# Causal mask of the exponentiated scores: sixteen extra contraction rows and a GpSimd select, replaced by one mask matmul for each diagonal block

## The reference, cut to what matters

```python
H, hd = 16, 16                        # B, T, D = 8, 1024, 256
q, k, v = split(h @ W_qkv)            # h: layer norm of x, scaled and shifted
attn = einsum('bhqd,bhkd->bhqk', q, k) / sqrt(hd)
attn = attn + where(key > query, -inf, -slope[h] * |key - query|)   # causal ALiBi
attn = softmax(attn, axis=-1)
x = x + ga * (einsum('bhqk,bhkd->bhqd', attn, v) @ W_out)
```

## Time and profile before

| | |
|---|---|
| median of 3 runs | 4325.94 us (4319.2 to 4332.71) |
| the profiled execution | 4325.94 us, its span 4324.2 us |
| busy in the span | PE 3432.9 us (79%), DVE 3542.9 (82%), ACT 2259.0 (52%), POOL 2620.2 (61%) |
| first and last `b_pT` score matmul | 306.0 and 1315.5 us |
| POOL selects L636 | 704 in number, 192.0 + 46.6 us busy |
| PE mask matmuls L676 | 1024, 218.3 us busy |

### The profile page before, as it was taken

How to read it: one execution, slowest core, us unless ns; L and a number is a source line. 1 busy time by engine, 2 the same in 40 slices (tenths; PEclk the granted TensorE clock), 3 DMA queues, 4 the chain that set the end, 5 groups by cost and what they waited for, 6 DMA issues and landing times. The chain is left out here.

```text
span 4324.2 us, 73212 instructions
## 1 busy us (share of the span) xinstructions
PE 3432.9 (79%) x22476; PEld 1607.5 (37%) x22476; DVE 3542.9 (82%) x5196; ACT 2259.0 (52%) x3974; POOL 2620.2 (61%) x2515
## 2 busy tenths in 40 slices
PE   5979999999994999999567777777777777777567
PEld 3634333344332555555222322222222222222156
DVE  5767777777754999999279999989999899998957
ACT  5626666666673333333355565656565555565422
POOL 1102222222221888887178888888898888888823
PEclk8979999999997999999778888778888888888589
DMA  4884554554522111110112222221222222212222
GB/s 146 285 153 67 82 78 66 79 81 66 82 38 80 35 47 42 46 45 25 47 43 53 67 52 66 63 49 47 66 67 56 66 53 67 56 50 46 53 86 86
DMA packets 274023, 300.44 MB, mean 69 GB/s; under 512 B 34560, under 2 KB 204663, under 8 KB 273623
## 3 DMA queue, kind: packets, MB, share of 16 engines
q1 hardware_dynamic: 273630, 295.68, 31.0%
HBM read 210.22 MB, written 84.51 MB: 68 GB/s over the span
## 5 line engine op out<-in xcount | busy, mean ns | idle before, releaser
L1684 POOL TENSOR_TENSOR d_dBu<-d_dtu,d_Bn 128x1024 f32<-128x1024 f32 x512 | 1202.9, 2375 | 184.9 <-DVE d_h L1751 184.8
L785 DVE TENSOR_REDUCE b_Gc<-b_pS 128x1 f32<-128x512 f32 (+4 forms) x1248 | 742.8, 644 | 228.7 <-PE b_pS L676 147.5
L1532 ACT ACTIVATE d_dA<-d_dt,d_decay 128x512 f32<-128x512 f32 x1024 | 690.2, 687 | 446.4 <-DVE d_h L1751 429.0
L758 ACT ACTIVATE b_P<-b_pT 128x512 f32<-128x512 f32 (+1 forms) x1120 | 572.3, 575 | 373.9 <-PE b_pT L664 371.7
L1751 DVE TENSOR_TENSOR_SCAN d_h<-d_dA,d_dBu 128x512 f32<-128x512 f32 x512 | 586.1, 1203 | 99.4 <-ACT d_dA L1532 92.2
L1751 DVE TENSOR_TENSOR_SCAN d_h<-d_dA,d_last_h,d_dBu 128x512 f32<-128x512 f32 x512 | 616.1, 1262 | 54.3 <-ACT d_dA L1532 51.4
L674 PE MATMUL b_pS<-KS,QS 99*128 99x512 bf16 (+3 forms) x1536 | 475.7, 339 | 47.6 <-DVE b_Gc L785 25.5
L636 POOL TENSOR_SCALAR_AFFINE_SELECT b_P<-b_P 128x128 f32<-128x128 f32 (+2 forms) x608 | 192.0, 323 | 527.5 <-ACT b_P L758 515.7
L664 PE MATMUL b_pT<-QS,KS 118*128 118x512 bf16 (+3 forms) x1536 | 450.8, 330 | 40.7 <-issue 21.3
L1758 DVE TENSOR_TENSOR d_h<-d_h,d_C 128x2048 f32<-128x2048 f32 x192 | 433.8, 2259 | 0.7 <-PE d_C L1415 0.7
L1487 PE MATMUL d_f<-d_xnT,w_inT 128*128 128x512 f32 x512 | 329.0, 777 | 127.6 <-DVE d_h1e L1818 61.2
(11 more groups left out here) (300 smaller groups left out, 5922.1 us busy)
## 6 DMA issues: line engine op xcount, KB each, us to landing
d_Bn<-scratch_bs SPq DMA_DIRECT2D x64, 1024.0 KB, 8.3
scratch_parts<-a_part SPq DMA_DIRECT2D x48, 512.0 KB, 4.0
QS<-scratch_parts SPq DMA_DIRECT2D x192, 128.0 KB, 7.0
KS<-scratch_parts SPq DMA_DIRECT2D x192, 128.0 KB, 7.4
scratch_v<-a_v SPq DMA_DIRECT2D x16, 1024.0 KB, 7.4
V<-scratch_v SPq DMA_DIRECT2D x32, 512.0 KB, 10.9
a_x<-in_L_attn_x_dram SPq DMA_DIRECT2D x16, 512.0 KB, 7.1
scratch_o<-b_O SPq DMA_DIRECT2D x16, 512.0 KB, 9.0
```

The lines of the kernel that those rows point to most:

```text
L758: act.activation(t[:, heads[0]:heads[-1] + 1, c * CH:c * CH + w], pT[:, place % RING, 0:len(heads) * w].rearrange("p (h w) -> p h w", w=w) ...
L785: dve.tensor_reduce(Gc[:, m.k % 2, c, :].rearrange("p (h t) -> p h t", t=QT)[:, heads[0]:heads[-1] + 1, qt], pS[:, j % RING, 0:len(heads) ...
L1532: act.activation(dA[:, m % 2, :], dt[:, c.k % 2, m, :], ACT.Exp, scale=decay[:, m, n:n + 1]).then_inc(dA_d, 1)
L1684: pool.tensor_tensor(dBu[:, n % 2, 2 * j:2 * j + 2, :], dtu[:, c.k % 2, 2 * j:2 * j + 2, :], Bn[:, n // BG % 2, n % BG, :].unsqueeze(1).to ...
```

## The change

The edge rows go (KROWS falls from 118 to 102) and with them their making in `setup`; ACT's two fills write ones from a single column instead. The POOL selects in `attend` go. In their place PE adds a mask to each diagonal block of `b_pT` by one matmul of `ident_bf` and a new constant `mask_kq`, into the same bank, before ACT exponentiates. The V products then wait for ACT's exponentials (`p_done`) instead of POOL's selects (`p_masked`).

```diff
-EDGE = 64
-NEDGE = T // EDGE
-KROWS = NROW + 2 * NPART + NEDGE
+KROWS = NROW + 2 * NPART
...
+            pool.memset(K["mask_kq"][:, :], 0.0).then_inc(id_set, 1)
...
-            q_edge, k_edge, own = edge[:, 0, :], edge[:, 1, :], (NROW + 2 * NPART) * EDGE
-            pool.wait_ge(edge_set, 2)
...
+            pool.affine_select(out=K["mask_kq"][:, :], in_=K["mask_kq"][:, :], compare_op=ALU.is_ge, fill=MASKED,
+                               base=0, pattern=[[-1, P]], channel_multiplier=1).then_inc(id_done, 1)
...
-            act.wait_ge(edge_set, 6)
-            for i, rows in enumerate((K["QS"], K["KS"])):
-                rows = rows[NROW:KROWS, :, :, :].rearrange("p g h t -> p (g h) t")
-                act.activation(rows, edge[NROW:KROWS, i, :].unsqueeze(1).to_broadcast(rows.shape), ACT.Copy).then_inc(ones, 1)
+            act.wait_ge(one_set, 1)
+            for rows in (K["QS"], K["KS"]):
+                rows = rows[NROW:KROWS, :, :, :].rearrange("p g h t -> p (g h t)")
+                act.activation(rows, one[NROW:KROWS, :].to_broadcast(rows.shape), ACT.Copy).then_inc(ones, 1)
...
-            dve.memset(edge[:, 0, :], MASKED).then_inc(edge_set, 1)
-            dve.memset(edge[:, 1, :], 1.0).then_inc(edge_set, 1)
-            dve.wait_ge(edge_set, 5)
-            dve.memset(edge[NROW:NROW + 2 * NPART, :, :], 1.0).then_inc(edge_set, 1)
+            dve.memset(one[:, :], 1.0).then_inc(one_set, 1)
...
-            def drop_masked(u, j):
-
-                i, c, heads, w = EXPS[j]
-                t = Ps[:, i - SMALL, :, :] if i >= SMALL else Pr[:, i % 2, :, :]
-                own = t[:, heads[0]:heads[-1] + 1, c * CH + w - P:c * CH + w]
-                wait_before(pool, p_done, u.times(NE_, j + 1), passed)
-                pool.affine_select(out=own, in_=own, compare_op=ALU.is_ge, fill=0.0,
-                                   base=0, pattern=[[0, len(heads)], [-1, P]], channel_multiplier=1).then_inc(p_masked, 1)
-
             def step(m, u):
                 joined = joined_before(m, u)
-                for j in range(NE_):
-                    if j == G_AT and joined is not None:
-                        split(joined)
-                    if u is not None and j in DIAGONALS:
-                        drop_masked(u, j)
+                if joined is not None:
+                    split(joined)
...
-                    last = pe.matmul(p, KS[0:KROWS, g, h, kt * P:(kt + 1) * P], QS[0:KROWS, g, h, c * CH:c * CH + w], start=True, stop=True)
+                    diagonal = c * CH + w == (kt + 1) * P
+                    last = pe.matmul(p, KS[0:KROWS, g, h, kt * P:(kt + 1) * P], QS[0:KROWS, g, h, c * CH:c * CH + w], start=True, stop=not diagonal)
+                    if diagonal:
+                        last = pe.matmul(p[:, w - P:w], K["ident_bf"][:, :], K["mask_kq"][:, :], start=False, stop=True)
...
-                    wait(pe, p_masked, u.times(ND, sum(EXPS[j][0] <= i for j in DIAGONALS)))
+                    wait(pe, p_done, u.times(NE_, sum(piece[0] <= i for piece in EXPS)))
```

More of the change, by code:

```diff
@@ L123, in setup @@
         alp = K["alp"]
-        al, alr, edge = sb("al", [P, P]), sb("alr", [P, 2, P]), sb("edge", [P, 2, T], BF16)
-        al_in, al_step, edge_set, ones = sem("al_in"), sem("al_step"), sem("edge_set"), sem("ones")
+        al, alr, one = sb("al", [P, P]), sb("alr", [P, 2, P]), sb("one", [P, 1])
+        al_in, al_step, one_set, ones = sem("al_in"), sem("al_step"), sem("one_set"), sem("ones")
         block = local.enter_context(nc.Block())
@@ L147, in _ @@
             pool.memset(K["mask_qk"][:, :], 0.0).then_inc(id_set, 1)
-            pool.wait_ge(id_set, 3)
+            pool.memset(K["mask_kq"][:, :], 0.0).then_inc(id_set, 1)
+            pool.wait_ge(id_set, 4)
             for t in ("ident", "ident_bf"):
@@ L154, in _ @@
                                base=0, pattern=[[1, P]], channel_multiplier=-1).then_inc(id_done, 1)
-            q_edge, k_edge, own = edge[:, 0, :], edge[:, 1, :], (NROW + 2 * NPART) * EDGE
-            pool.wait_ge(edge_set, 2)
[L158 to L166, removed]
+            pool.affine_select(out=K["mask_kq"][:, :], in_=K["mask_kq"][:, :], compare_op=ALU.is_ge, fill=MASKED,
+                               base=0, pattern=[[-1, P]], channel_multiplier=1).then_inc(id_done, 1)
+            pool.wait_ge(id_done, 4)
         @block.scalar
@@ L531, in attend @@
         g_put = [sem(f"g_put{g}") for g in range(NG)]
-        t_mm, p_done, p_masked, pv_done, passed = sem("t_mm"), sem("p_done"), sem("p_masked"), sem("pv_done"), sem("passed")
+        t_mm, p_done, pv_done, passed = sem("t_mm"), sem("p_done"), sem("pv_done"), sem("passed")
         oT_out, o_tr, r_done, o_done, o_st = sem("oT_out"), sem("o_tr"), sem("r_done"), sem("o_done"), [sem("o_st0"), sem("o_st1")]
@@ L562, in attend @@
         LAST = At(B - 1, NG, NG - 1)
[L564 to L570, removed]
         def weights(i, h, c, w):
@@ L2085, in kept @@
             return {n: stack.enter_context(nc.sbuf_tensor(n, shape, dt)) for n, (shape, dt) in shapes.items()}
-        K = kept(ctx, {"ident": ([P, P], F32), "ident_bf": ([P, P], BF16), "mask_qk": ([P, P], BF16),
+        K = kept(ctx, {"ident": ([P, P], F32), "ident_bf": ([P, P], BF16), "mask_qk": ([P, P], BF16), "mask_kq": ([P, P], BF16),
                        "sa0": ([P, KD, B], F32), "ca0": ([P, KD, B], F32), "sb1": ([P, KD, B], F32), "cb1": ([P, KD, B], F32)})
```

## The result

| | before | after |
|---|---|---|
| median | 4327.55 us (4319.2 to 4332.71, 4 runs) | 4370.9 us (4369.94 to 4378.83, 4 runs) |
| ratio, 95% interval | | 1.0106 (1.0086 to 1.0127) |
| profiled execution, its span | 4325.94, 4324.2 us | 4365.23, 4363.5 us |
| busy PE, DVE, ACT, POOL | 3432.9, 3542.9, 2259.0, 2620.2 us | 3482.9, 3543.0, 2274.2, 2380.8 us |

The change costs 43 us by the medians (37 to 55 us by the interval); 4374 us was forecast. POOL lost 239 us of work and PE gained 50 us of busy time, and the end moved by about PE's share.

A forecast was written before the change was run, and what follows sets the result against it. PE was taken to bound attention; 49.2 us for masks in 30 paired units, 0 for the tail, -0.5 for `setup` and 0 for the loop gave +48.7 on 4325.94, so 4374 us, range 4354 to 4392 (8 in 10).

The forecast's parts named there:

- PE sets the pace, POOL doesn't: Attention units: PE busy 29.73 to 30.56 of 31.09 us, POOL about 9; V products no longer waiting for POOL costed at nothing.
- 0.059 us a mask: Price of each new 128-column mask matmul on PE, from start to start; ends 0.055 and 0.063 us.
- the longest rival: Mask's weight load in attention units does not hide: 0.098 us a mask, +83 us, about 4408 us; chance 0.06 with prices between.
- the rule that the prediction weighed: Sustained weight load and matmul pairs on PE: about 81 ns per 128-column matmul, making the time about 4394 us.
- Which 29 count: Of 32 masks a unit, pieces 4, 5 and 12 vanish in PE's waits; 29 count, 1.64 us a unit, +49.2 us.
- Tail 0: Last two units, without maxima half: selects' removal and added masks together 0, ends -1.3 and +2.5 us.
- Its two terms: Last two units: selects removed, some -1.3 us; 64 masks added, +1.3 us out of 0 to 3.8.
- Loop's return 0: Six PE idle times at the loop's return, 21.3 us in sum, taken not to grow; +3.7 us if growing with the body.
- Setup -0.5: In `setup`, ACT's fills start sooner without DVE's edge fill: -0.9 us or 0, taken as -0.5.
- The masks falling into idle time: PE's 0.54 + 0.82 us idle a unit takes masks up: +16 us, 4341 us; chance 0.06, parts of it included.
- ACT setting the pace: ACT's releases, not PE, pace attention: masks free, V products one POOL hop earlier, about -20 us, 4306 us; chance 0.03.
- no effect: Attention: masks' cost and selects' removal both hidden, the change does nothing, 4326 us; chance 0.02.

The follow-up runs named there:

- both: Kernel before with the 32 new mask matmuls a unit added on PE, POOL's selects and edge rows kept; 4376.11 us, ratio 1.0121.
- nomask: Kernel before without POOL's selects and the wait for them, no mask matmuls in their place, edge rows kept; 4320.77 us, ratio 0.9994.
- halfmask: Kernel before with the 32 mask matmuls of the maxima cut from 128 to 64 columns; 4311.88 us, ratio 0.9972.
- early: Kernel before without POOL's selects, new mask matmul only in pieces 4, 5 and 12; 4327.29 us, unit 31.09 us.
- chain: Kernel before without POOL's selects, new mask matmul only in pieces 6 and 7; 4326.24 us, unit 31.21 us.
- two: Kernel after with each new mask matmul issued twice in a row, 64 a unit; 4431.74 us, ratio to before 1.0257.
- slopemask: Kernel before with masks of the maxima kept only for heads 0 and 1, at 64 columns; 4301.12 us, ratio 0.9932.

## Why the prediction was right

- *PE sets the pace, POOL doesn't.* Shown by both and nomask: with masks, 32.72 to 32.73 us a unit whether POOL selects or not; without masks, 31.09 whether it does or not. That holds for the units; in the tail POOL's hop was on the path (below).
- *0.059 us a mask.* Shown: 0.058 in the rows after; 1.61 us for the second 29 is 0.056 each. The unit grew by 1.63 us for 1.64 forecast. The 98 ns weight load (the longest rival) did not show, and halfmask, with the same load and half the columns, has the price at 0.03. By the rule that the prediction weighed (the Trainium skill, TensorE: Matmul & The Clock Gate, Back-to-back issue gap), the page's 81 ns would have made a unit of 33.4 us, an estimate; the trace after disagrees with that figure too, and comes near the 56 ns that the page gives for the gap without a load, though every mask here has one.
- *Which 29 count.* Shown for the first 5 of the 32 by early and chain, and for the other 27 by the 1.60 us that the unit after has gained behind piece 12. One detail was off: I expected the wait for `b_gT` to fall by 0.12 to 0.42 us, it fell to 0.46. Before, the score of piece 5 came 0.46 us after that of piece 4, where scores of 512 columns take 0.22 each; a few hundredths of idle time stood there, and the mask of piece 4 filled those first.
- *Tail 0.* Right as a sum, by luck: from the last `b_gT` to the next stage 54.4 us before and 54.7 after. Its two terms were both too small. Taking the selects away is worth 2.0 us there (nomask), or 1.6 with the masks in place (both has 56.2), for 1.3 forecast; the masks cost 1.8 (both) to 2.3, for 1.3 forecast. The errors cancel.
- *Loop's return 0.* Right within what it varies by: the six units there grew by 1.79 us on the mean where others grew by 1.63, 0.9 us in all. Both, with the same masks, shows 4.72 us over an ordinary unit, less than the 5.27 of before. Growth with the body is not shown; the stretch at the 1.2 GHz level behind a return decides more.
- *Setup -0.5.* At one of its ends, and for another reason. ACT's fills did end 2.5 us sooner (33.66 for 36.20), but they weren't what set the end. From the issue of the store to the next stage's first transfer it is 4.4 us in both kernels:

```profile
33.02 0.38 SPq L136 DMA_DIRECT2D scratch_mod<-mod_sb  x1
37.44 0.39 SPq L288 DMA_DIRECT2D a_wqkv<-in_L_attn_W_qkv_dram  x1
```

  before, 33.95 to 38.38. The chain ahead of the store was 0.9 us shorter because the first twelve `psM` matmuls took 6.92 us for 7.68. In two, which has the same `setup` as the kernel after, they took 7.74, the store is issued at 33.79 and the stage ends at 38.21: the edge rows' going gave nothing that can be told from this variation. Nor does the start of `attend` tell: 1.5 us sooner in the kernel after, where 0 to 1 was forecast, 0.3 in two, and 1.2 in slopemask, whose `setup` is that of before.
- *Rivals.* The masks falling into idle time (4341), ACT setting the pace (4306) and no effect are all excluded by the unit of 32.72 us and by both and nomask.

## What to carry to other kernels

Before work is moved from an engine with slack to the one that sets the pace, walk one period of that engine: price the new instruction by start-to-start distance in a row of the same kind, and for each wait ask whether the instruction comes ahead of something that the wait hangs on. Only work ahead of a wait that ends by someone else's chain is free. The same arithmetic, turned round, finds the gain: here the masks to work on were those already on TensorE, and narrowing or dropping them, where a bound on the row maximum does as well as the maximum, gave 0.3% and 0.7%, while VectorE became the next bound. And where two small terms have opposite signs, as in the tail here, a right sum says nothing about either: run each alone.

## What the runs showed of the hardware

Between two returns of the loop the pipeline repeats its period to 0.01 us over a thousand microseconds and over chips (31.09 us in before, nomask and early), but for the unit behind a return, while the stages behind it varied by 15 us for the same code. So a change of 0.1 us in a period of 31 could be read from one profile each, which no comparison of times could have done. A `b_pT` mask of 128 columns costs the same from start to start behind a load of other weights (0.058 us) as behind a load of the same ones (0.055 to 0.06), and one of 64 columns about 0.03, though each load is shown as 98 ns. Behind the idle time at the loop's return TensorE's granted clock fell to the 1.2 GHz level in all returns of the nine kernels but one; in both, the unit of that one took 35.9 us, those with such a stretch 37.5 to 38.0.
